# Spare matmuls of constants on TensorE in the first steps of a vision tower kernel

## What is computed

```python
def _L0_tok_ref(x, ...):
    q, k, v = proj(Wq_w, Wq_b), proj(Wk_w, Wk_b), proj(Wv_w, Wv_b)
    ew, ek = jnp.exp(w_bias * local_mask), jnp.exp(k)
    num = jnp.einsum('ts,nsd->ntd', ew, ek * v)
    den = jnp.einsum('ts,nsd->ntd', ew, ek)
    h = (jax.nn.sigmoid(q) * num / den) @ out_w + out_b + _flatten(x)
    ...  # layer norm with ln_g, ln_b

def _L0_attn_ref(x, ...):
    a_t = jax.nn.sigmoid(log_a) * jax.nn.sigmoid(x @ W_r + b_r)
    b_t = (1.0 - a_t) * jax.nn.sigmoid(x @ W_i + b_i) * (x @ W_in + b_in)
    ...  # h = a_t * h + b_t over the sequence
    return h @ W_out + b_out

h = _L0_tok_ref(x, ...)
h = concatenate([cls_tok, h])
h = h + _L0_attn_ref(_layernorm(h), ...)
h = h + _L0_ffn_ref(_layernorm(h), ...)   # shared expert + gate * expert, two of eight
```

## Time and profile before

| | before |
|---|---|
| median of three runs | 1067.86 us |
| profiled execution | 1067.47 us |
| its span | 1065.7 us |
| mean granted TensorE clock | 0.955 |
| TensorE busy with matmuls | 970.7 us, 91% of the span |
| VectorE busy | 705.3 us, 66% |
| ScalarE busy | 454.7 us, 43% |
| GpSimd busy | 378.0 us, 35% |

### The profile page before, as it was taken

One profiled execution on the slowest core, in us unless ns is written; L12 is line 12 of the kernel. 1 busy time (PEld: TensorE's weight loads), 2 busy tenths in 40 slices (PEclk: granted clock), 3 DMA queues, 4 the chain that ended last, 5 costly groups with the idle time before them and its releaser, 6 DMA issues.

```text
span 1065.7 us, 21605 instructions
## 1 busy us (share of the span) xinstructions
PE 970.7 (91%) x6889; PEld 899.1 (84%) x6890; DVE 705.3 (66%) x2095; ACT 454.7 (43%) x1139; POOL 378.0 (35%) x468
## 2 busy tenths in 40 slices
PE   5787788999999999999788999999999999999995
PEld 3555587888888888888787899999999999999995
DVE  3458788887887877888776446464645546564643
ACT  2011143344444444444332255555555555555553
POOL 4232554242343243343421133443243424243222
PEclk9667799999999999999999799999999999999998
DMA  9300610111100111100011372837272633664322
GB/s 275 104 10 11 173 40 1 40 42 40 40 20 22 38 40 40 40 20 15 32 45 41 122 202 45 208 52 190 40 212 45 168 79 80 163 129 126 45 40 31
DMA packets 48164, 82.68 MB, mean 78 GB/s; under 512 B 6416, under 2 KB 30883, under 8 KB 48132
## 3 DMA queue, kind: packets, MB, share of 16 engines
q0 software_dynamic: 31056, 57.46, 22.3%
q1 hardware_dynamic: 17076, 24.84, 7.9%
HBM read 55.32 MB, written 26.96 MB: 77 GB/s over the span
## 4 chain that ended last, share of the span: by engine, by line
PE 41%; issue 27%; DVE 15%; POOL 13%; ACT 1%; POOLq 1%; DMA 0%; DVEq 0%; SPq 0%; ACTq 0%
PE ps_nd L657 14%; PE ps_proj L642 8%; POOL out L603 5%; PE ps_proj L722 5%; PE ps_ri L642 4%; DVE rden L1254 3%; PE ps_ip L642 3%; POOL v_rows L498 2%; PE ps_nd L843 2%; POOL h L561 1%; PE ps_h L830 1%; PE ps_h L815 1%; POOL rstd L494 1%; PE ps_t L729 1%; DVE A L1386 1%
## 5 line engine op out<-in xcount | busy, mean ns | idle before, releaser
L1077 DVE TENSOR_TENSOR GL<-g_act,GH 128x256 fp32r<-128x256 f32 (+1 forms) x424 | 185.3, 439 | 189.4 <-ACT GH L955 170.3
L657 PE MATMUL ps_nd<-w2h,GH 128*128 128x256 f32 x832 | 248.9, 299 | 24.9 <-DVE GL L1077 13.5
L950 ACT ACTIVATE g_act<-ps_proj,fcb 128x256 f32<-128x256 f32 (+1 forms) x280 | 130.8, 468 | 308.8 <-PE ps_proj L642 300.6
L657 PE MATMUL ps_nd<-w2l,GH 128*128 128x256 f32 x832 | 235.8, 283 | 0.0
L657 PE MATMUL ps_nd<-w2h,GL 128*128 128x256 f32 x832 | 234.7, 282 | 0.0
L657 PEld LDWEIGHTS ps_nd<-w2h,GH 128*128 128x128 f32 x832 | 158.4, 190 | 35.2 <-DVE GL L1077 14.0
L955 ACT CAST GH<-g_act 128x256 fp32r<-128x256 f32 x416 | 161.4, 397 | 0.0
L657 PEld LDWEIGHTS ps_nd<-w2l,GH 128*128 128x128 f32 x832 | 158.8, 191 | 0.0
L657 PEld LDWEIGHTS ps_nd<-w2h,GL 128*128 128x128 f32 x832 | 158.1, 190 | 0.0
L642 PE MATMUL ps_proj<-xh,w1h 128*128 128x256 f32 x544 | 116.3, 295 | 9.3 <-issue 4.4
L603 POOL DMA_INDIRECT out<-yb,rows_to x72 | 114.8, 1595 | 16.7 <-issue 12.8
(11 more groups left out here) (271 smaller groups left out, 1943.4 us busy)
## 6 DMA issues: line engine op xcount, KB each, us to landing
R<-v_rows SPq DMA_DIRECT2D x37, 260.0 KB
w1h<-fc_w POOLq DMA_DIRECT2D x9, 1024.0 KB
w2h<-pj_w POOLq DMA_DIRECT2D x9, 1024.0 KB
stage<-fc_w POOLq DMA_DIRECT2D x9, 1024.0 KB
stage<-pj_w POOLq DMA_DIRECT2D x9, 1024.0 KB
v_rows<-tail_rows SPq DMA_DIRECT2D x16, 260.0 KB, 3.0
x<-x SPq DMA_DIRECT2D x16, 256.0 KB, 3.6
out<-yb SPq DMA_DIRECT2D x16, 256.0 KB, 2.1
```

Of the source, the lines that this page charges most:

```text
L657: last = pe.matmul(banks[a], g[:, j, a * P:(a + 1) * P], w[i][:, j, :], start=(j == 0 and q == 0), stop=(j == HT - 1 and q == 2))
L950: act.activation(g_act[:, j % G_SLOTS, 0:width], banks[j % len(banks)][:, 0:width], ACT.Gelu_apprx_tanh, bias=fcb[i][:, j:j + 1]).then_inc ...
L1077: dve.tensor_tensor(GL[:, j, 0:width], g_act[:, j % G_SLOTS, 0:width], GH[:, j, 0:width].bitcast(F32), ALU.subtract).then_inc(gl_done, 1)
```

## The change

A helper `spare(count, bank)` issues f32 matmuls of `ones_pp` with itself, 128 columns each, into a bank of PSUM whose contents nobody needs at that point. It is called at eleven points of steps 0 to 3, with 3 to 9 matmuls each, 59 in all. The wait for `consts` moves from step 1 to the very start, ahead of the first group, since `ones_pp` must be there.

```diff
+            def spare(count, bank):
+
+                for _ in range(count):
+                    pe.matmul(bank, ones_pp[:], ones_pp[:], start=True, stop=True)
+
+            pe.wait_ge(consts, CONSTS)
+            spare(9, ps_h[:, 0, 0:P])
             pe.wait_ge(proj_loaded, 16)
             pe.wait_ge(ones_in_x, 2)
 
             def step(t, par):
+                if isinstance(t, int) and t == 2:
+                    spare(7, ps_ip[:, 0, 0:P])
                 if live(t):
                     project(t, par, 0)
+                if isinstance(t, int) and t < 2:
+                    spare(3, ps_h[:, 0, 0:P])
                 if live(t - 1):
                     n = t - 1
-                    if isinstance(n, int) and n == 0:
-                        pe.wait_ge(consts, CONSTS)
                     pe.wait_ge(y_ready, n + 1)
...
+                if isinstance(t, int) and t == 1:
+                    spare(3, ps_h[:, 0, 0:P])
                 if live(t):
                     project(t, par, 1)
+                if isinstance(t, int) and t == 0:
+                    spare(3, ps_h[:, 0, 0:P])
...
                     if j == 6 and isinstance(t, int) and t == 1:
+                        spare(7, ps_ri[:, 1, 0:P])
                         cls_a()
+                    if j == 7 and isinstance(t, int) and t in (2, 3):
+                        spare(5, ps_proj[:, 0, 0:P])
                     if j == 7 and live(t - 1):
                         transpose_u(t - 1)
                 if isinstance(t, int) and t == 1:
+                    spare(5, ps_proj[:, 0, 0:P])
                     cls_b()
                 if isinstance(t, int) and t == 2:
+                    spare(9, ps_proj[:, 0, 0:P])
                     cls_c()
```

## The result

| | before | after |
|---|---|---|
| median | 1067.71 us (1067.48 to 1068.58, 4 runs) | 1061.67 us (1059.2 to 1062.03, 4 runs) |
| ratio | | 0.9935, 95% interval 0.9922 to 0.9949 |
| span of the profiled execution | 1065.7 us | 1060.0 us |
| mean granted clock | 0.955 | 0.968 |
| clock in the first 125 us | 0.74 | 0.81 |

The change took 6.0 us off between the medians; by the ratio 5.4 to 8.3 us. Forecast were 4.5 us and 1063.4 us.

What follows compares the result with a forecast made beforehand. Time to win lay in steps 0 to 4, where TensorE's clock is low; later work was a fixed block. -2.8 - 2.7 + 1.0 = -4.5 us, so 1067.86 - 4.5 = 1063.4 us; range 1057.5 to 1067.5.

Steps and rivals of the forecast that it cites:

- The price of a spare: Each 128-column matmul of ones on TensorE: 0.43 us at 1.2 GHz, 0.22 us at 2.4 GHz, priced from ps_nd.
- The transpose's price: Lower price considered for one spare, from a transpose of the same size: 0.24 us slow, 0.16 us fast.
- Start: -2.8: Step 0: 9 spares delay the first projection 1.4 us; faster projections and ps_nd's first half gain 4.2 us.
- Step 1: -2.7: 3 + 3 spares around the transposes of Y hold the clock; projection gains 1.78 us, ps_h about 1.0; else 0.
- End of step 1 and step 2: Groups of 7 and 5 at step 1's end, 7 in step 2: cost taken as 0, no gain booked.
- Where the rises fall: +1.0: Everything behind step 1: later clock rises may miss chain work; +1.0 us booked between -11.3 and +3.4.
- The fixed block: Work once the experts' matmuls fill TensorE, after steps 0 to 4: only starts earlier or later, keeping the lead.
- stay at ps_nd: Rival, 17%: spares and projections don't raise the clock before ps_nd; 0 or -1.3 us, about 1067 us.
- hold throughout: Rival, 15%: clock holds nearly throughout, work behind step 1 gains half its bound too; -11.1 us, about 1057 us.
- given back later: Rival, 11%: the first two gains come, later rises cost the full +3.4 us; -2.1 us, about 1065.8 us.
- The plain load: Rival, 8%: spares never fast; +1.4 us at start, +0.5 in step 2, +1.7 for a late rise; about 1071.5 us.

Runs made afterwards that it cites:

- the first group alone: Changed kernel with only the 9 spares at the start and the moved wait, other ten groups removed: 1070.32 us, ratio 1.0004.
- steps 0 and 1 alone: Changed kernel keeping the groups 9, 3, 3, 3 and 3, without the six later groups: 1064.95 us, ratio 0.9968.
- dense: Changed kernel plus spares in its bare waits, among the class token's gates and more in step 1: 1054.88 us, ratio 0.9887.
- the narrow spares: Changed kernel with all 59 spares streaming 2 columns in place of 128, same weights and places: 1069.26 us, ratio 1.0006.
- the filled waits: Changed kernel with spares also in the waits it left bare in steps 1, 2 and 4: 1057.2 us, ratio 0.9896.

## Why the prediction was right

**The price of a spare** was right: 4.0 us for nine slow ones (0.44, taken 0.43); 0.83 us for three fast ones with their tail. The transpose's price was no match.

**Start: -2.8.** In the first profile -2.77: 1.5 late, first projection 2.54, second 2.21, ps_nd's first half 1.97. The term was right for that execution. As a worth in the median it was not: without the first group the full change keeps its time. So the sum met the median partly by luck, for 2.8 of its 4.5 us stand on a term that the medians don't show. I had priced the group with the rise in the middle of the first projection and taken for granted that it holds; the first group alone shows the fall in one bare wait of 1.56 us.

**Step 1: -2.7.** In the first profile it was exactly that, 5.50 - 2.77 us. In the second the clock fell. I had written "I take the clock to hold ... if it falls all the same, 0"; both happen.

**End of step 1 and step 2.** I had booked 0 for the gates; they took 7.81 us again (5.98 in the profile without the first group). The five and the seven spares delayed nothing: the seven took 1.97 us, in place of the 3.0 that I had feared. The clock was up behind them: the projection that follows took 2.14 us, and 3.80 in the profile that has neither group (steps 0 and 1 alone). The gain in step 2 was 1.0 us.

**Where the rises fall: +1.0.** Up to the first matmul of the shared expert it was +2.1 in the first profile (lead 5.5 to 3.35; 131.99 to 128.64), in the two places named: ps_h of step 3, and projection and ps_h of step 4, which had caught the rise in before. The sign was right, the size half.

**The fixed block** was the step that failed. I took everything from the shared expert on as a block that only shifts. But its clock falls at other places too: at 570 and 587 us in before and not in after, and the lead went from 3.35 to 5.7 us at the end. The sum was saved by it: -5.5 + 2.1 - 2.3 = -5.7 in the span. That these later falls went after's way in the profiled execution is luck; nothing in the change aims at them. In other profiles the same stretch, from h of step 4 to the end, took 1.2 us off the lead (the first group alone), changed nothing (dense) or added 2.1 (steps 0 and 1 alone).

**The rivals.** The rise did not stay at ps_nd, nor did it hold throughout; "given back later" is what the first profile shows at 126 us, and was undone later. The plain load is what the narrow spares show: 0.9 us slower between medians and 2.5 in the span of the profiled execution, against the 3.6 that I had computed with a late rise added.

The page "TensorE: Matmul & The Clock Gate" of the Trainium skill (Part 1, "The HAM clock gate") says that the number of slow matmuls at the start varies from run to run of one kernel. The prediction said that the four executions shown (within 1.1 us) bore little of it out. More runs do: 35 of before range from 1066.64 to 1071.99 us, six of after from 1059.32 to 1065.58, and two profiles of after differ in the clock of one projection and the ps_h behind it. At the start, the projection behind the same nine spares took 2.14, 2.54 and 3.62 us in three of the profiles (the first group alone, after, the filled waits).

## What to carry to other kernels

Where TensorE's wide work comes in bursts with waits between, look at how long equal matmuls take at different places before counting columns or calls. Put spares into the waits right ahead of work on the chain: here a group at the very start that is followed by bare waits gave nothing, and filling the last bare waits gave almost as much again as the whole change. Use full-width matmuls: two-column ones kept TensorE as busy and gained nothing. Such a gain is a chance in each execution, so it takes many runs, not one trace, to size it.

## What the runs showed of the hardware that I had not expected

- Behind nine wide f32 matmuls in 3.7 us the next projection ran fast (2.14 us), and behind one bare wait of 1.56 us the one after it ran slow (3.77 us). It is not certain: in the profile of the filled waits the projection behind the same nine took 3.62 us.
- Matmuls of two columns with full 128 by 128 weights held TensorE for 4.00 us and left the clock down (3.76 us for the projection behind them), where the 128-column ones raised it.
- A fall of the clock cost time where TensorE was on the chain and none where it was not: the one at 150 us left the lead at 3.5 us, those at 570 and 587 us moved it by 1.2 and 1.1.
- The clock of a stretch differs between executions of the same kernel: 3.39 and 2.21 us for the same projection behind the same wait of 1.1 us.
